# Window attention and a two-of-eight expert mixer on one core: attention scores in 32-row tiles, two units at a time

## The reference, cut to what matters

```python
x = x + conv(_ln_c(x))        # conv: window attention
t = tokens(x)                 # (B, 16384, 64)
t = t + ffn(_ln_t(t))         # ffn: top 2 of 8 experts

# conv, per window of N = 64 tokens, nh = 4 heads of dh = 16
xw = x.reshape(B, H // 8, 8, W // 8, 8, C).transpose(0, 1, 3, 2, 4, 5).reshape(-1, N, C)
q, k, v = xw @ Wq + bq, (xw @ Wkv + bkv)   # split by head
attn = softmax(einsum('bhnd,bhmd->bhnm', q * dh ** -0.5, k) + rel_bias[index])
out = einsum('bhnm,bhmd->bhnd', attn, v) @ Wproj + bproj

# ffn, per token
p = softmax(x @ router_w + router_b); top_p, top_i = top_k(p, 2); top_p /= top_p.sum()
y = sum_k top_p[k] * (x @ expert_w[top_i[k]] + expert_b[top_i[k]])
```

## Time and profile before

| | |
|---|---|
| time of the runs | 1578.07 us (1576.57 to 1578.12) |
| the profiled execution: its time, its span | 1576.16 us, 1574.4 us |
| PE busy | 1419.0 us, 90% |
| PE weight loads | 893.7 us, 57% |
| DVE busy | 1223.4 us, 78% |
| ACT busy | 1025.6 us, 65% |
| POOL busy | 890.6 us, 57% |
| mean granted clock | 0.991 of full |

### The profile page before, as it was taken

One profiled execution on the slowest core, in us unless ns is written; L12 is line 12 of the kernel. 1 busy time (PEld: TensorE's weight loads), 2 busy tenths in 40 slices (PEclk: granted clock), 3 DMA queues, 4 the chain that ended last, 5 costly groups with the idle time before them and its releaser, 6 DMA issues.

```text
span 1574.4 us, 44468 instructions
## 1 busy us (share of the span) xinstructions
PE 1419.0 (90%) x15211; PEld 893.7 (57%) x15360; DVE 1223.4 (78%) x2742; ACT 1025.6 (65%) x1928; POOL 890.6 (57%) x733
## 2 busy tenths in 40 slices
PE   4489999989998999989998999998999999999976
PEld 3265656656665665655665665665666556655641
DVE  7558889887776888887777788888777777777764
ACT  5477777757666767756665776775676666666631
POOL 0255555578654555559755555557955555665542
PEclk9999999999999999999999999999999999999998
DMA  5012233222212223312212323322221222122221
...
DMA packets 95213, 89.99 MB, mean 57 GB/s; under 512 B 26653, under 2 KB 62173, under 8 KB 95070
## 3 DMA queue, kind: packets, MB, share of 16 engines
q1 hardware_dynamic: 95070, 88.17, 24.0%
...
## 4 chain that ended last, share of the span: by engine, by line
PE 73%; DVE 12%; issue 7%; POOL 3%; ACT 3%; DMA 1%; SPq 1%; DVEq 0%; ACTq 0%; POOLq 0%
PE bank L516 14%; PE bank L380 12%; PE bank L404 10%; PE bank L505 6%; PE bank L419 5%; DVE t_g L960 4%; PE bank L432 4%; PE bank L459 4%; PE bank L447 3%; PE bank L497 2%; PE bank L476 2%; PE bank L493 2%; PE bank L390 2%; DVE sums L806 2%; PE bank L469 1%
## 5 line engine op out<-in xcount | busy, mean ns | idle before, releaser
L1052 POOL TENSOR_TENSOR prob<-prob,mx 128x512 f32<-128x512 f32 x256 | 266.9, 1043 | 340.4 <-DVE mx L856 340.4
L960 DVE TENSOR_TENSOR t_g<-t_t,bank 128x512 f32<-128x512 f32 x384 | 262.9, 685 | 163.7 <-PE bank L505 162.8
L516 PE MATMUL bank<-t_g,w_exp 128*64 128x512 f32 x1024 | 273.8, 614 | 16.8 <-DVE t_g L960 8.4
L404 PE MATMUL bank<-k_m,q_bd 128*128 128x256 f32 x1024 | 274.6, 392 | 10.2 <-ACT q_bd L633 5.5
L380 PE MATMUL bank<-xn,w_qkv 128*64 128x256 f32 x1536 | 210.8, 395 | 23.8 <-POOL xn L1046 17.7
L404 PEld LDWEIGHTS bank<-k_m,q_bd 128*128 128x128 f32 x1024 | 180.4, 193 | 76.4 <-issue 55.1
L505 PE MATMUL bank<-g_t,gate_sel 128*128 128x512 bf16 x426 | 165.7, 389 | 46.9 <-DVE t_g L960 44.1
L850 DVE TENSOR_TENSOR prob<-bank,rel 128x512 f32<-128x512 f32 x256 | 175.5, 686 | 33.8 <-PE bank L404 24.5
L1043 POOL TENSOR_TENSOR xn<-xt,rstd 128x512 f32 (+1 forms) x64 | 81.3, 1270 | 196.0 <-PE bank L380 193.9
L641 ACT ACTIVATE k_m<-bank,k_bias,k_mask 128x512 f32<-128x512 f32 x256 | 183.6, 772 | 8.8 <-PE bank L380 8.8
L1074 POOL TENSOR_TENSOR t_g<-t_t,g_copy 128x512 f32<-128x512 f32 x128 | 165.0, 1289 | 39.2 <-ACT g_copy L692 39.2
...
## 6 DMA issues: line engine op xcount, KB each, us to landing
t_t<-t_rout SPq DMA_DIRECT2D x256, 128.0 KB, 3.7
...
out_y<-y_out SPq DMA_DIRECT2D x128, 128.0 KB, 2.3
...
```

The source lines that it names most:

```text
L404: last = mm(B_S[i % 2][:, n * 256:(n + 1) * 256], q_bd[:, p, w, :], k_m[:, p, w, :, :].rearrange("p h k -> p (h k)"), start=True, stop=Tru ...
L516: mm(B_Y[C * a:C * a + C, :], w_exp[:, pair, :], t_g[:, (2 * pair + a) % TG, :], start=False, stop=(pair == MIXES // 2 - 1), skip_group_ch ...
L960: V.tensor_tensor(t_g[:, u % TG, :], t_t[:, p, u % 2, :], B_G[:, :], ALU.mult).then_inc(tg_dve.sem, 1)
L1052: G.tensor_tensor(sc, sc, mx[:, i, :].unsqueeze(2).broadcast_to([P, 2 * HEADS, NTOK]), ALU.subtract).then_inc(s_shifted.sem, 1)
```

## The change

The scores are made in tiles of 32 rows by 64 columns. `q_bd` is replaced by `q_t` (no zeros, half the size), `k_m` has two copies instead of four, each with every other head at zero, so that 32 rows hold two heads. A window and a pair of heads is one matmul of 32 rows, 64 columns and 128 moving elements (two heads by 64 keys). `scores(g, p, pair)` does two units in one go, 16 matmuls, in the order unit, window pair, window, pair of heads. The four tiles that follow each other lie in four groups of rows; the two tiles with the same columns write to different banks. The two score banks are now one tensor that a call fills whole, so `pair` waits for the bias of the pair before it. VectorE's bias and maxima are separate functions of 1024 elements each; `rel` is stored twice as long. `copy_q` is two copies of all 128 rows, `copy_k` two copies a strip.

The orders of the slots change with it. On TensorE the scores stand at two places instead of four: pair 1 at the slot's start, and pair 0 of the next strip between the gates 3 and 4. `turn_probs` 1 stands behind `turn_tokens`, or, where there is a `take`, behind `logits`. Then come gate 4, `turn_probs` 2, the second `take`, `project` 2, `experts` 1, gate 5, `turn_probs` 3, gate 6, `project_out`. On VectorE the routing steps 0 to 8 are in one piece, bias and maxima of the next strip stand around gate 4, `normalise` stands behind gate 5, and gate 7 ahead of `statistics` and `add_input`. On ScalarE `exps` 3 moves ahead of `copy_q`, and `exps` 0 of the next strip to the slot's end; on GpSimd `shift` 1 of the next strip moves to the slot's end, ahead of `centre_tokens`. The two memsets of `q_bd` at the start go. The diff's core (indentation reduced):

```diff
 
 
 xn = sb("xn", [P, 4, H])
-q_bd = sb("q_bd", [P, 2, PAIRS, 2 * NTOK])
-k_m = sb("k_m", [P, 2, PAIRS, HEADS, NTOK])
+q_t = sb("q_t", [P, 2, PAIRS, NTOK])
+k_m = sb("k_m", [P, 2, PAIRS, 2, NTOK])
 v_t = sb("v_t", [P, UNITS, 2, NTOK])
 v_bd = sb("v_bd", [P, 2, UNITS, 2, HEADS, 2 * DH])
 ones_bd = sb("ones_bd", [P, 2 * DH])
...
 
-bank = [ctx.enter_context(nc.psum_tensor(f"bank{i}", [P, BANK], F32)) for i in range(8)]
-B_S = bank[0:2]
-B_T = bank[2]
-B_O = bank[3]
-B_E = bank[4]
-B_P = bank[5]
-B_G = bank[6]
-B_Y = bank[7]
+B_S = ctx.enter_context(nc.psum_tensor("bank_s", [P, 2, 2, 2, 2, NTOK], F32))
+B_T, B_O, B_E, B_P, B_G, B_Y = (
+ctx.enter_context(nc.psum_tensor(f"bank_{n}", [P, BANK], F32)) for n in "toepgy")
 
...
-def scores(g, p, i):
-
-    if i == 0:
-        pe.wait_ge(q_ready.sem, q_ready.at(g, 4))
-        pe.wait_ge(k_ready.sem, k_ready.at(g, HEADS))
-    if i >= 2:
-        pe.wait_ge(s_biased.sem, s_biased.at(g, i - 1))
-    elif not (isinstance(g, int) and g == 0):
-        pe.wait_ge(s_biased.sem, s_biased.at(g - 1, i + 3))
-    for n in range(2):
-        w = UNITS * n + i
-        last = mm(B_S[i % 2][:, n * 256:(n + 1) * 256], q_bd[:, p, w, :], k_m[:, p, w, :, :].rearrange("p h k -> p (h k)"),
-                  start=True, stop=True, skip_group_check=True)
+def scores(g, p, pair):
+
+    if pair == 0:
+        pe.wait_ge(q_ready.sem, q_ready.at(g, 2))
+        pe.wait_ge(k_ready.sem, k_ready.at(g, 2))
+    if not (isinstance(g, int) and g == 0 and pair == 0):
+        pe.wait_ge(s_biased.sem, s_biased.at(g, pair))
+    for i in range(2):
+        for n in range(2):
+            for b in range(2):
+                for hp in range(2):
+                    rows = slice(C * b + 2 * DH * hp, C * b + 2 * DH * hp + 2 * DH)
+                    w = UNITS * n + 2 * pair + i
+                    last = mm(B_S[C * b:C * b + C, hp, i, :, n, :], q_t[rows, p, w, :], k_m[rows, p, w, :, :],
+                              start=True, stop=True, skip_group_check=True)
     last.then_inc(s_done.sem, 1)
...
     if attending:
-        scores(j, p, 2)
+        scores(j, p, 1)
...
         turn_tokens(j - 2)
     if work.take:
         take(work.batch, *work.take, 0, j)
-    if attending:
-        scores(j, p, 3)
+    if attending and not work.take:
         turn_probs(j, 1, work)
     if mixing:
         gates(j - 3, 1)
     if routing_on:
         logits(j - 2)
+    if attending and work.take:
+        turn_probs(j, 1, work)
     if mixing:
         gates(j - 3, 2)
     if projecting:
@@ -552,23 +550,23 @@
     if mixing:
         experts(j - 3, 0)
         gates(j - 3, 3)
-    if attending:
-        turn_probs(j, 2, work)
-    if mixing:
-        gates(j - 3, 4)
     if projecting:
         scores(j + 1, 1 - p, 0)
     if mixing:
-        gates(j - 3, 5)
+        gates(j - 3, 4)
+    if attending:
+        turn_probs(j, 2, work)
     if work.take:
         take(work.batch, *work.take, 1, j)
     if projecting:
         project(j + 1, 2)
     if mixing:
         experts(j - 3, 1)
+        gates(j - 3, 5)
+    if attending:
+        turn_probs(j, 3, work)
+    if mixing:
         gates(j - 3, 6)
-    if attending:
-        turn_probs(j, 3, work)
     if outputting:
         project_out(j - 1)
     if mixing:
@@ -576,7 +574,6 @@
         experts(j - 3, 2)
     if projecting:
         turn_values(j + 1, attending)
-        scores(j + 1, 1 - p, 1)
     if mixing:
         experts(j - 3, 3)
...
     act.wait_ge(qkv_done.sem, qkv_done.at(g, 2))
-    for ab in range(2):
-        rows = slice(C * ab, C * ab + C)
-        for half in range(2):
-            A(q_bd[rows, p, :, ab * NTOK:(ab + 1) * NTOK].rearrange("p v (r l a) -> p v r l a", a=2, l=4)[
-                :, :, :, :, half],
-              turned(B_P[rows, 256 * half:256 * half + 256]), ACT.Identity, bias=q_bias[rows, :],
-              scale=float(DH) ** -0.5).then_inc(q_ready.sem, 1)
-
-def copy_k(g, p, heads):
+    for half in range(2):
+        A(q_t[:, p].rearrange("p v (r l a) -> p v r l a", a=2, l=4)[:, :, :, :, half],
+          turned(B_P[:, 256 * half:256 * half + 256]), ACT.Identity, bias=q_bias[:, :],
+          scale=float(DH) ** -0.5).then_inc(q_ready.sem, 1)
+
+def copy_k(g, p, e):
     act.wait_ge(qkv_done.sem, qkv_done.at(g, 1))
-    for h in heads:
-        A(k_m[:, p, :, h, :].rearrange("p v (a l) -> p v a l", l=4), turned(B_P[:, :]), ACT.Identity,
-          bias=k_bias[:, h:h + 1], scale=k_mask[:, h:h + 1]).then_inc(k_ready.sem, 1)
+    A(k_m[:, p, :, e, :].rearrange("p v (a l) -> p v a l", l=4), turned(B_P[:, :]), ACT.Identity,
+      bias=k_bias[:, e:e + 1], scale=k_mask[:, e:e + 1]).then_inc(k_ready.sem, 1)
 
...
 def slot(j, p, work, on):
     projecting, attending, outputting, routing_on, mixing = stages(on)
-    if attending:
-        exps(j, 0)
     if routing_on:
         square(j - 2)
+    if attending:
+        exps(j, 1)
     if outputting:
         copy_sums(j - 1)
     if attending:
         copy_probs(j, 0)
     if mixing:
         copy_turned_gates(j - 3)
-    if attending:
-        exps(j, 1)
     if projecting:
-        copy_k(j + 1, 1 - p, (0, 1))
+        copy_k(j + 1, 1 - p, 0)
+        copy_k(j + 1, 1 - p, 1)
     if routing_on:
         copy_tokens(j - 2)
     if work.take:
-        take(work.batch, *work.take, 0, B_T)
-    if projecting:
-        copy_k(j + 1, 1 - p, (2, 3))
+        take(work.batch, *work.take, 0, B_T[:, :])
     if attending:
         copy_probs(j, 1)
         exps(j, 2)
     if mixing:
         copy_gates(j - 3, 2)
+    if attending:
+        exps(j, 3)
     if projecting:
         copy_q(j + 1, 1 - p)
     if attending:
-        exps(j, 3)
         copy_probs(j, 2)
     if work.take:
         square_planes(work.batch, *work.take, 0)
     if routing_on:
         gate_exp(j - 2)
     if work.take:
-        take(work.batch, *work.take, 1, B_T)
+        take(work.batch, *work.take, 1, B_T[:, :])
     if projecting:
         copy_v(j + 1)
+    if attending:
+        copy_probs(j, 3)
     if mixing:
         copy_gates(j - 3, 6)
-    if attending:
-        copy_probs(j, 3)
     if work.take:
         square_planes(work.batch, *work.take, 1)
     if projecting:
+        exps(j + 1, 0)
         spread_values(j + 1, 1 - p)
     if mixing:
...
 
-def bias_and_max(g, i):
-    dve.wait_ge(s_done.sem, s_done.at(g, i + 1))
-    V.tensor_tensor(
-        prob[:, i].rearrange("p h n k -> p n h k"),
-        B_S[i % 2][:, :].rearrange("p (n h k) -> p n h k", n=2, h=HEADS),
-        rel[:, :].rearrange("p (h k) -> p h k", h=HEADS).unsqueeze(1).broadcast_to([P, 2, HEADS, NTOK]),
-        ALU.add).then_inc(s_biased.sem, 1)
-    dve.wait_ge(s_biased.sem, s_biased.at(g, i + 1))
-    V.tensor_reduce(mx[:, i, :], prob[:, i].rearrange("p h n k -> p (h n) k"), AX.X,
+def bias(g, pair):
+    dve.wait_ge(s_done.sem, s_done.at(g, pair + 1))
+    V.tensor_tensor(prob[:, 2 * pair:2 * pair + 2].rearrange("p i (g e) n k -> p g i (e n k)", e=2),
+                    B_S[:, :, :].rearrange("p g i e n k -> p g i (e n k)"),
+                    rel[:, :].rearrange("p (g s) -> p g s", g=2).unsqueeze(2).broadcast_to(
+                        [P, 2, 2, HEADS * NTOK]), ALU.add).then_inc(s_biased.sem, 1)
+
+def maxima(g, pair):
+    dve.wait_ge(s_biased.sem, s_biased.at(g, pair + 1))
+    V.tensor_reduce(mx[:, 2 * pair:2 * pair + 2, :].rearrange("p i s -> p (i s)"),
+                    prob[:, 2 * pair:2 * pair + 2].rearrange("p i h n k -> p (i h n) k"), AX.X,
                     ALU.max).then_inc(mx_ready.sem, 1)
...
     projecting, attending, outputting, routing_on, mixing = stages(on)
     if attending:
-        bias_and_max(j, 1)
+        bias(j, 1)
     if routing_on:
         token_variance(j - 2)
     if attending:
-        bias_and_max(j, 2)
+        maxima(j, 1)
     if work.sums:
         sum_planes(work.batch, *work.sums)
     if mixing:
@@ -977,31 +971,28 @@
         sum_squares(work.batch, *work.sums)
     if mixing:
         gate(j - 3, 1 - p, 1)
-    if attending:
-        bias_and_max(j, 3)
     if routing_on:
-        routing(j - 2, 0, 4)
+        routing(j - 2, 0, 8)
     if mixing:
         gate(j - 3, 1 - p, 3)
-    if routing_on:
-        routing(j - 2, 5, 8)
+    if projecting:
+        bias(j + 1, 0)
     if mixing:
         gate(j - 3, 1 - p, 4)
+    if projecting:
+        maxima(j + 1, 0)
+    if mixing:
+        gate(j - 3, 1 - p, 5)
     if outputting:
         normalise(j - 1)
-    if mixing:
-        gate(j - 3, 1 - p, 5)
-    if projecting:
-        bias_and_max(j + 1, 0)
     if routing_on:
         routing(j - 2, 9, 13)
+    if mixing:
+        gate(j - 3, 1 - p, 7)
     if work.up:
         statistics(work.batch)
     if outputting:
         add_input(j - 1, 1 - p)
-    if mixing:
-        gate(j - 3, 1 - p, 7)
-    if outputting:
         token_mean(j - 1, 1 - p)
     if routing_on:
...
 
 def shift(g, i):
-    pool.wait_ge(mx_ready.sem, mx_ready.at(g, i + 1))
```

(7 more changed lines are left out.)

48 lines of the change are left out of this document (22 added, 26 removed).

## The result

The changed kernel takes 1584.41 us (median of 11 runs, 1580.99 to 1587.26) where the kernel before takes 1576.57 beside it (11 runs): ratio 1.0053, interval 1.004 to 1.0066. It is 8 us slower; the forecast was 6 us faster. The time lies inside the forecast range of 1525 to 1625, but the change went the other way. The profiled execution took 1585.95 us with a span of 1584.1.

A forecast was written before the change was run, and what follows sets the result against it. TensorE was taken as nearly full, and after the change a loop through VectorE, GpSimd and the gates as the bound. 1576.2 -20 (plain) +18 (takes) +4 (powers) -8 (filling, draining) = 1570 us; range 1525 to 1625.

The forecast's parts named there:

- the pair, 1.0 us: Scores on TensorE: a pair in row tiles takes some 1.0 us, 2.0 a slot, where four units took 4.3 a slot.
- Rival C: Slower: the row tiles' weight loads don't overlap, a pair takes 1.9 us, +99 us, 1670; chance 0.10.
- second price for a pair, 1.1: Scores on TensorE: by the skill page's 3.07 times, not 4, a pair takes about 1.1 us, 0.2 a slot more.
- 4.3: Upper bound for a pair of scores on TensorE, in us, if no two tiles overlap.
- the length of the loop, 21.5 to 21.6: Plain slot: waits through VectorE, GpSimd and the gates, from `turn_tokens` to the next, sum to 21.5 to 21.6 us.
- the takes, 24.0: Slots with a take: 21.5 + 0.8 + 0.4 + 1.3 = 24.0 us, 0.75 more than before.
- The waits named: TensorE: about 0.5 us before `logits`, 0.5 for gate 5's product, 0.4 for `normalise`, 0.9 for `copy_probs` in takes.
- 24 slots with a take, +18: The 24 slots with a take each get 0.75 us longer, +18 us together.
- there are 31 full ones: -20: Plain slots: each of 31 full ones gains some 0.65 us, -20 us together.
- the power slots' +4: Nine slots where GpSimd has two powers: 0.5 us more each, from between 0 and 1, +4 us.
- eight filling and draining slots: -8: Filling and draining: TensorE and ScalarE wait less for q, k and scores, 1 us each, -8 us.
- Rival D: Slower: new waits in takes and power slots are larger, 1 us more in 33 slots, 1587 to 1630; chance 0.20.

The follow-up runs named there:

- run 1: Changed kernel with `normalise` ahead of gate 5 on VectorE, and maxima behind gate 5: 1578.1 us, ratio to the kernel before 0.9992.
- run 5: Changed kernel's order without the tiles: 128-row matmuls, four k and four q copies, two biases a pair, two memsets: 1731.05 us, 1.0976.
- run 7: Changed kernel with the second pair of scores ahead of `experts` 3 of the slot before: 1583.41 us, ratio to the kernel before 1.0037.
- run 6: Changed kernel with unread matmuls while TensorE waits, ahead of `experts` 3 in third power slots and `turn_tokens` in the drain: 1581.16 us, 1.0017.

## Why the prediction was wrong

**Right: the pair, 1.0 us.** It took 1.03 to the next group. Rival C, weight loads that don't overlap, is out. The prediction's second price for a pair, 1.1, is a slip in its working; the last section has the 1.4 that its own 4.3 gives.

**Right: the length of the loop, 21.5 to 21.6, and of the takes, 24.0.** Measured 21.3 (405.5 / 19) and 24.0 (503.2 / 21). The waits named are there: 0.51 ahead of the logits' weights, 0.44 for gate 5's product, 0.78 for `B_T`, and 0.21 for `normalise`, half of what was expected. But run 1 took the wait for `normalise` away, and the plain slots stayed as long. So the length came out right, and that this link sets it is not shown: VectorE's own queue takes over from it at once.

**Right: 24 slots with a take, +18.** They gave +17.5: +12.2 in the 21, +0.6 in the second filling slot, +4.7 in the two batch starts. The last is in part chance, since 0.75 each was forecast for the starts and 2.35 came: the rest is a second gap and a longer stretch at low clock (run 5), which no term has.

**Wrong: "there are 31 full ones: -20", with the power slots' +4.** The prediction doesn't say which 31. Nineteen plain slots, three with statistics and nine with powers make 31, and these gave -12.3 for the -16: -15.7, -3.3 and +6.7. The three with the last sums, which no term counts, gave +1.3. In the first two power slots of a batch GpSimd is busy 19.9 of 22.0 us and waits another 1.9 for the variance, so TensorE's gain isn't theirs (+0.1 each). The third took +2.0, of which 1.1 is the clock after TensorE's stand for gate 6 (run 7). That is 5 us of the error of 15.7 (+9.7 in span, -6 forecast).

**Wrong, and most of the error: "eight filling and draining slots: -8".** They and the ends gave +3.2 (+2.3 in the first filling slot, -0.9 in the drain, +1.8 at the ends), 11 us off. No row stood behind this term, and it left out the clock. Three of the four draining slots do gain, 1.1 to 1.4 each, as told. In the last, TensorE fell to the half clock (0.78 in the window, 1.00 before), and it took 2.7 us more; keeping TensorE busy gave 2.1 of them back (run 6). The first filling slot ran at 0.83 for the 1.00 of before. Its length varied from 17.8 to 20.9 us over the kernels with tiles, so its share and that of the ends are known to a few us only.

So what the change brought was summed right where its waits were read, and it fell short where another limit held: the clock where TensorE stands longer than before, and GpSimd's own work. Rival D named the power slots as a danger and priced them among the takes, where there was none.

**The change's moves.** With TensorE's old order, the other engines keeping the new one, the tiles take 1702 us, so some of TensorE's moves are needed. The old order on all engines with the tiles wasn't tried. Two things in the new order are not: gate 5 behind `experts` 1 costs 24 us, and the take ahead of `project` 2, right behind `turn_probs` 2, costs 17. Without these two the same change is 2.3% faster than the kernel before.
